# Down projection of a fused cross-attention and expert layer: Strassen's seven products for the second half of each turned group's sum

## The reference, cut to what matters

```python
x = x + attention(layernorm(x), ctx)          # 16 x 112 tokens, 256 wide
h_in = layernorm(x)
# 8 experts, each 256 -> 1024 -> 256, every token goes through all of them
g = jnp.einsum('bsh,ehf->ebsf', h_in, w_gate)
u = jnp.einsum('bsh,ehf->ebsf', h_in, w_up)
h = jax.nn.silu(g) * u
expert_out = jnp.einsum('ebsf,efh->ebsh', h, w_down)
out = jnp.einsum('ebsh,bse->bsh', expert_out, cw)   # cw: one share per token and expert
x = x + out
```

## Time and profile before

| | |
|---|---|
| median of 3 runs | 964.24 us (963.97 to 976.44) |
| the profiled execution | 965.87 us, its span 963.9 us |
| PE busy | 959.1 us, 100% of the span, 5090 matmuls |
| PE weight loads | 890.0 us, 92% |
| DVE, ACT, POOL busy | 541.0, 615.3 and 642.4 us: 56%, 64%, 67% |
| granted TensorE clock | 1.000 |

### The profile page before, as it was taken

How to read it: one execution, slowest core, us unless ns; L and a number is a source line. 1 busy time by engine, 2 the same in 40 slices (tenths; PEclk the granted TensorE clock), 3 DMA queues, 4 the chain that set the end, 5 groups by cost and what they waited for, 6 DMA issues and landing times.

```text
span 963.9 us, 14994 instructions
## 1 busy us (share of the span) xinstructions
PE 959.1 (100%) x5090; PEld 890.0 (92%) x5090; DVE 541.0 (56%) x1024; ACT 615.3 (64%) x1109; POOL 642.4 (67%) x536
## 2 busy tenths in 40 slices
PE   9999999999999999999999999999999999999998
PEld 7999899999999999999999999999999999999998
DVE  4998455455555655556555565555555555555564
ACT  6988556666666566666666566666666565666662
POOL 5899975956566665766565675667565656757564
DMA  7462412311001110111010110111100110112035
GB/s 194 141 157 82 126 60 72 112 46 60 23 23 44 42 64 22 45 41 42 23 44 23 42 63 23 45 41 42 45 23 22 43 61 23 45 42 67 14 53 139
DMA packets 73233, 55.85 MB, mean 58 GB/s; under 512 B 30244, under 2 KB 69485, under 8 KB 73158
## 3 DMA queue, kind: packets, MB, share of 16 engines
q1 hardware_dynamic: 73150, 54.91, 19.6%
q10 hardware_dynamic: 8, 0.00, 0.0%
HBM read 46.58 MB, written 6.48 MB: 55 GB/s over the span
## 4 chain that ended last, share of the span: by engine, by line
PE 97%; DVE 1%; DMA 1%; ACT 0%; issue 0%; SPq 0%; DVEq 0%; ACTq 0%
PE ps L355 95%; PE ps L1874 1%; DMA xf<-in_L_xattn_Wk 1%; PE ps L1910 0%; PE ps L1862 0%; PE ps L1927 0%; DVE early L1371 0%; ACT arena L892 0%; DVE xsacc L1562 0%; PE ps L1953 0%; PE ps L1820 0%; ACT xf L900 0%; ACT xf L892 0%; ACT early L879 0%; DVE ps L1553 0%
## 5 line engine op out<-in xcount | busy, mean ns | idle before, releaser
L355 PE MATMUL ps<-arena 128*128 128x448 f32 (+5 forms) x2064 | 388.3, 339 | 0.1
L355 PEld LDWEIGHTS ps<-arena 128*128 128x128 f32 (+2 forms) x2064 | 343.7, 187 | 21.0 <-DVE arena L366 0.4
L702 POOL TENSOR_TENSOR arena<-shared,arena 128x448 fp32r<-128x448 f32 x196 | 223.8, 1160 | 190.7 <-ACT arena L1107 186.8
L355 PE MATMUL ps<-xc_hi,w_hi 128*128 128x448 f32 x904 | 330.8, 366 | 0.1
L355 PE MATMUL ps<-xc_hi,w_lo 128*128 128x448 f32 x904 | 330.2, 365 | 0.0
L355 PE MATMUL ps<-xc_lo,w_hi 128*128 128x448 f32 x904 | 330.2, 365 | 0.0
L355 PEld LDWEIGHTS ps<-xc_hi,w_hi 128*128 128x128 f32 x904 | 169.8, 188 | 14.0 <-DVE ps L1496 0.5
L355 PEld LDWEIGHTS ps<-xc_hi,w_lo 128*128 128x128 f32 x904 | 169.8, 188 | 13.6
L355 PEld LDWEIGHTS ps<-xc_lo,w_hi 128*128 128x128 f32 x904 | 169.9, 188 | 13.1
L1107 ACT CAST arena<-shared 128x448 fp32r<-128x448 f32 x180 | 102.2, 568 | 108.4 <-DVE shared L1521 44.0
L1553 DVE TENSOR_TENSOR ps<-ps,xf 128x448 f32<-128x448 f32 x104 | 65.6, 631 | 146.3 <-PE ps L355 146.3
(11 more groups left out here) (171 smaller groups left out, 1068.1 us busy)
## 6 DMA issues: line engine op xcount, KB each, us to landing
early<-in_L_ffn_w_down SPq DMA_DIRECT2D x16, 512.0 KB, 3.9
xf<-cw_dram SPq DMA_DIRECT2D x16, 448.0 KB, 4.6
shared<-in_ctx SPq DMA_DIRECT2D x16, 336.0 KB
w_raw<-in_L_ffn_w_gate SPq DMA_DIRECT2D x17, 256.0 KB, 2.7
w_raw<-in_L_ffn_w_up SPq DMA_DIRECT2D x17, 256.0 KB, 3.1
early<-in_L_ffn_w_gate SPq DMA_DIRECT2D x15, 256.0 KB, 2.7
early<-in_L_ffn_w_up SPq DMA_DIRECT2D x15, 256.0 KB, 3.1
xsacc<-in_x SPq DMA_DIRECT2D x8, 224.0 KB, 6.1
```

The costliest lines, as they stand in the source:

```text
L355: ins = nc.tensor.matmul(dst, w, m, start=first and i == 0, stop=last and i == len(passes) - 1, skip_group_check=onto)
L702: nc.gpsimd.tensor_tensor(h[:, 1, j, at:at + TC], tile, h[:, 0, j, at:at + TC].bitcast(fp32), ALU.subtract).then_inc(hid_lo_done, 1)
```

## The change

The hidden tile that quad `n = 2g+1` adds to the down projection of a turned group is a 256 x 896 block (two blocks by two), and so is the result. The change makes its share with Strassen's seven products of three passes, and leaves the first quad's share plain (24 passes).

- **PE.** The four units of a group become nine pieces: `down_1` (3 passes), `down_c11` (3+6), `down_6` (3), `down_7` (3), `down_5` (3) in the even quad, `down_c12` (3+6) and `down_c21_c22` (3+6+6) in the odd one.
- **Sums of the hidden blocks.** DVE makes S3, S1 and S2 (`sums_of_hidden`, each waiting for the one before) once hidden21 is there; hidden21 itself now stays in the PSUM bank `u_x`, and so does S1. POOL makes S4. ACT and POOL split S2, S3 and S4, and ACT and DVE split S1 (`high_sum`, `low_sum`, `low_s1`). Only blocks 11, 12 and 22 of the second quad are split as they are.
- **Sums of the down weights.** POOL makes four (`sum_of_down`); eleven slots instead of eight are split, in two steps (a and b).
- **Keeping and seeding.** ACT seeds one bank with product 1 and keeps products 2 and 5 (`down_seed`, `down_keep2`, `down_keep5`), DVE adds them (`down_c12`, `down_c22`).
- The gate and up weight sums are laid out in seven slots for eight, one weight copy is made whole, the blocks in the arena have other places, and two row tiles of group 1 move to the end of quad 5.

```diff
+            def sums_of_hidden(n):
+                made = 3 * (n // FPAIRS - CP)
+                ve.wait_ge(hid_done, 4 * n + HID21)
+                nc.vector.tensor_tensor(g21, g11, u_x, ALU.subtract).then_inc(s_sum, 1)
+                ve.wait_ge(s_sum, made + S3_MADE)
+                nc.vector.tensor_tensor(u_x, u_x, g22[1], ALU.add).then_inc(s_sum, 1)
+                ve.wait_ge(s_sum, made + S1_MADE)
+                at_least(ve, s_lo_done, made)
+                nc.vector.tensor_tensor(s2_tile, u_x, g11, ALU.subtract).then_inc(s_sum, 1)
...
             def up_seed(n):
                 sc.wait_ge(hid_done, 4 * n)
+                if summed(n - 1):
+                    sc.wait_ge(s1_lo_done, (n - 1) // FPAIRS - CP + 1)
...
+            def high_sum(n, k, src, at):
+                g = n // FPAIRS
+                if k == S4_HI:
+                    sc.wait_ge(s4_made, g - CP + 1)
+                else:
+                    sc.wait_ge(s_sum, 3 * (g - CP) + S2_MADE)
...
+                nc.scalar.copy(single[at][:, 0, :], src).then_inc(s_hi_done, 1)
+            def down_keep5(g):
+                sc.wait_ge(down_prod, piece(g, D_P5))
+                at_least(sc, down_sum, 2 * (g - CP))
+                nc.scalar.copy(d_p5, ps_unit[0]).then_inc(down_kept, 1)
```

ACT's quad, the part that the prediction speaks of:

```diff
+                if odd and turned:
+                    down_keep5(g)
                 gate_seed(n)
                 gate_keep5(n)
                 up_seed(n)
...
+                if summed(n):
+                    high_hidden(n, HID12, g12[n % 2])
+                    activate21(n)
+                    high_hidden(n, HID22, g22[n % 2])
+                else:
+                    high_hidden(n, HID22, g22[n % 2])
+                    high_hidden(n, HID12, g12[n % 2])
+                    activate21(n)
+                    high_hidden(n, HID21, g21)
+                if turn == 3 and hn + 1 < SETS:
+                    high_set(2 * hn + 3)
+                if summed(n):
+                    high_sum(n, S1_HI, u_x, S1_AT)
+                    high_sum(n, S2_HI, s2_tile, S2_AT)
```

DVE's quad:

```diff
                 hidden22(n)
+                if not odd and g in TURNED:
+                    weigh(g, 0)
                 up_c12(n)
                 hidden12(n)
...
-                if not odd and g in TURNED:
-                    weigh(g, 0)
                 hidden21(n)
+                if summed(n):
+                    sums_of_hidden(n)
+                if odd and g in TURNED:
+                    weigh(g, 2)
```

PE's quad and two of the new functions:

```diff
                 if odd and turned:
-                    unit(g, 2)
+                    down_c12(g)
                 gate_6_2(n)
                 if odd and by_tile:
                     down(g, 3)
                 up_6_2(n)
+                if not odd and turned:
+                    down_1(g)
                 gate_7_3(n)
+                if not odd and turned:
+                    down_c11(g)
                 up_7_3(n)
...
                 if not odd and turned:
-                    unit(g, 0)
+                    down_6(g)
                 gate_4(n)
                 up_4(n)
                 if odd and turned:
-                    unit(g, 3)
+                    down_c21_c22(g)
                 if not odd and turned:
-                    unit(g, 1)
+                    down_7(g)
+                    down_5(g)
...
+            def down_5(g):
+                pe.wait_ge(s1_lo_done, g - CP + 1)
+                pe.wait_ge(unit_done, UNITS * (g - CP) + 1)
+                accumulate(ps_unit[0], summed_down(DT1, S1_AT)).then_inc(down_prod, 1)
+            def down_c12(g):
+                pe.wait_ge(s_lo_done, 3 * (g - CP) + S4_LO)
+                pe.wait_ge(down_kept, 3 * (g - CP) + D_KEPT5)
+                accumulate(ps_unit[0], summed_down(DB22, S4_AT) + plain_down(g, 0, 1), first=False, onto=True).then_inc(down_prod, 1)
```

More of the change, by code:

```diff
@@ L147, in xattn_ffn_kernel @@
         cw_all = xf_f[:, 0:CP * TH].rearrange("p (c t) -> p c t", c=CP)
+        d_u2, d_p5 = [xf[:, 4 + i, :] for i in range(2)]
         xc_hi = sb("xc_hi", [P, CP, 7, TC], fp32r)
@@ L797, in _ @@
             plain_low(1, 3)
[L798 removed]
+            low_down_first()
             low_part(0, "s4")
@@ L819, in quad @@
                 hn, turn = n // (CP * FPAIRS), n % (CP * FPAIRS)
-                if n > PLAIN:
-                    low_hidden(n - 1, HID21, g21, 0, TC)
-                if turn == 2:
-                    low_down(hn)
+                if n > PLAIN and not summed(n - 1):
+                    low_hidden(n - 1, HID21, g21)
                 if n == PLAIN:
@@ L1275, in quad @@
                 hn, turn = n // (CP * FPAIRS), n % (CP * FPAIRS)
+                g, odd = n // FPAIRS - 1, n % FPAIRS
+                turned = g in TURNED
+                if turn == 2 and hn == 1:
+                    high_down_a(hn)
+                if odd and turned:
+                    down_keep5(g)
                 gate_seed(n)
@@ L1784, in quad @@
                     turn(1, 1)
-                if not odd and g - 1 not in TURNED:
-                    add_rows(g - 1, 6, ps_r[6])
                 hidden11(n)
@@ new lines, in row_passes, with plain_down @@
+                passes = []
+                for j in range(2):
+                    h, t = pair_of(FPAIRS * g + fp, j), 2 * (2 * fp + 1 - j)
+                    passes += three(h[:, 0, toks], h[:, 1, toks], wd[:, t:t + 2, 0, :], wd[:, t:t + 2, 1, :])
+                return passes
+            def plain_down(g, r, d):
+                passes = []
+                for j, k in enumerate(((HID11, HID12), (HID21, HID22))[r]):
+                    h, t = block_of(FPAIRS * g, k), 2 * (1 - j) + d
+                    passes += three(wd[:, t, 0, :], wd[:, t, 1, :], h[:, 0, :], h[:, 1, :])
+                return passes
@@ new lines, in summed_down, with down_1 @@
+            def summed_down(slot, at):
+                h = single[at]
+                return three(wd[:, slot, 0, :], wd[:, slot, 1, :], h[:, 0, :], h[:, 1, :])
+            def down_1(g):
+                pe.wait_ge(wd_done, g // CP * 2)
+                pe.wait_ge(hid_lo_done, split_count(FPAIRS * g + 1, HID11))
+                if g == CP:
+                    pe.wait_ge(acc_done, RT * CP)
+                    prime(ps_unit[1])
+                at_least(pe, unit_done, UNITS * (g - CP))
+                accumulate(ps_unit[0], summed_down(DB11, A11_AT)).then_inc(down_prod, 1)
@@ L2284, in quad @@
                     down(g, 2)
-                if not odd and g - 1 not in TURNED:
+                if n == PLAIN:
                     down(g - 1, 5)
                 up_1_5(n)
-                if not odd and g - 1 not in TURNED:
+                if n == PLAIN:
                     down(g - 1, 6)
                 if odd and turned:
-                    unit(g, 2)
+                    down_c12(g)
                 gate_6_2(n)
```

405 lines of the change are left out of this document (271 added, 134 removed).

## The result

| | before | changed |
|---|---|---|
| median | 964.11 us (963.8 to 976.44, 4 runs) | **1003.51 us** (1002.8 to 1003.84, 4 runs) |
| ratio | | 1.040, 95% interval 1.037 to 1.044 |
| profiled execution, its span | 965.87, 963.9 us | 1002.8, 1000.7 us |
| PE, DVE, ACT, POOL busy | 959.1, 541.0, 615.3, 642.4 us | 958.4, 634.0, 657.8, 780.0 us |

What follows compares the result with a forecast made beforehand. PE was taken to bound the kernel, with 97% of the last chain. Per group -0.61 (passes) + 0.92 + 0.87 (two waits) = +1.18 us, times 28 = +33 us, giving 997 us against the 964.24 median, range 968 to 1014.

Steps and rivals of the forecast that it cites:

- Passes saved: On PE, three passes fewer in each of 28 groups, 84 x 0.2026 = 17.0 us, all on the path.
- Wait A: PE at the even quad's gate_6_2 waits for gate_seed, behind ACT's casts of S1 and S2: 0.92 us every group.
- Wait B: PE at the odd quad's down_c12 waits for down_keep5, behind the cast of block 21: 0.87 us every group.
- The other waits: At down_7, down_c11, down_5 and up_4: met with 0 to 0.4 us to spare; nothing taken for them.
- the one-time changes: Two tiles of group 1, first split of the larger weight set, sum for waits from group 2: -2 to +3 us.
- The row tiles' moving operand in two pieces: Row tiles' 256 columns now come in two pieces: 336 passes, up to 2 us in all.
- POOL as the bound: Rival: POOL late by 0.5 us at down_c11 and gate_1_5 in each group, 1025 us; chance 18%.
- Load of ACT: ACT gains three casts and three copies, about 3.4 us a group, making it about 78% busy.
- the pace of a pass: Every PE pass was taken to cost 0.2026 us, from the distances between unit starts.
- the prediction's last rival: New gaps drop PE's clock to 1.2 GHz, passes cost twice as much: at worst 732 us more; chance 1%.

Runs made afterwards that it cites:

- Experiment 10: Kernel before with the last pass of units 1, 2 and 3 of each turned group left out (84 passes, result incomplete): 947.34 us, ratio 0.982.
- Experiment 2: Changed kernel with ACT's casts of S1 and S2 moved behind the next quad's gate_seed and gate_keep5: 993.47 us, ratio 1.030.
- Experiment 3: Changed kernel with down_keep5 moved on ACT to the even quad, ahead of the cast of block 12: 992.13 us, ratio 1.028.
- Experiment 4: Experiment 3's kernel with ACT's splits high_down_a (turn 1) and high_set (turn 3) also moved behind up_keep2: 978.77 us, ratio 1.015.
- experiment 7: Changed kernel with one more 448-column GpSimd instruction, result unused, behind the split of S3 in each even quad: 1003.03 us, ratio 1.040.
- Experiment 1: Kernel before with the last three passes of unit 0 left out in each turned group (84 passes, result incomplete): 958.35 us, ratio 0.993.
- experiment 5: Changed kernel with the moves of Experiment 2 and Experiment 4 together: 966.99 us, ratio 1.003.
- experiment 6: Experiment 5's kernel with the second instruction of weigh(g, 2) moved behind low_s1 on DVE: 962.49 us, ratio 0.997.
- experiment 11: Experiment 6's kernel with the second step of the down split moved earlier in turn 2 on ACT and POOL: 958.85 us, ratio 0.995.
- experiment 12: Experiment 11's kernel with DVE making S1 then S2, and GpSimd making S3 as block 22 less S2: 957.79 us, ratio 0.993.
- experiment 8: Experiment 6's kernel with DVE making S1 and S2 first and S3 afterwards, as block 22 less S2 behind low_s1: 1058.12 us, ratio 1.098.

## Why the prediction was right

The forecast was 997 us with 968 to 1014 as range, slower with 76%; it came to 1003.5.

- **Passes saved: right.** Experiment 10 gives 16.8 us for 17.0, and not the 15.9 that the figure of the Trainium skill would give. (Its interval, 16 to 19 us, only just leaves out the 15.9; the distance of the starts, 0.2026 us, does so clearly.)
- **Wait A: right in place and cause, and near in size.** Forecast 0.92 a group, measured 0.75 to 1.07, 23.8 us in 28 against 25.8. Experiment 2 takes it away and leaves B. The chain in the timelines of ACT and DVE (against the earlier trace rows):

```profile
589.10 0.63 DVE L1672 TENSOR_TENSOR ps<-ps,shared 128x448 f32<-128x448 f32 x1
...
592.81 0.63 DVE L1697 TENSOR_TENSOR ps<-shared,ps 128x448 f32<-128x448 f32 x1 [1.08 <-ACT shared L1213]
593.47 0.62 DVE L1703 TENSOR_TENSOR shared<-shared,ps 128x448 f32<-128x448 f32 x1
594.13 0.63 DVE L1705 TENSOR_TENSOR ps<-ps,g_odd 128x448 f32<-128x448 f32 x1
594.79 0.62 DVE L1708 TENSOR_TENSOR shared<-ps,shared 128x448 f32<-128x448 f32 x1
```

```profile
595.45 0.53 ACT L1246 CAST arena<-ps 128x448 fp32r<-128x448 f32 x1 [0.63 <-DVE shared L1708]
595.88 0.57 ACT L1246 CAST arena<-shared 128x448 fp32r<-128x448 f32 x1
596.35 0.54 ACT L1157 COPY ps<-ps 128x448 f32<-128x448 f32 x1
```

  Counted from `down_c12`'s first matmul at 582.57, where the prediction's clock stood at 2.43: up_c22 came 6.53 later (forecast 6.33), hidden21 10.24 (10.03), S1 11.56 (11.35), S1's cast 12.88 (12.67), the seed 13.78 (13.61), PE's restart 14.37 (14.29). Every link has the forecast length to 0.1; the start is 0.2 later, since up's product ended later: the step after the restart is 0.08 longer than a pass, and 30 passes at the slower pace add 0.12.
- **Wait B: right, but for the first two groups.** Forecast 0.87, measured 0.84 to 1.30 in 26 groups, mostly 0.95, and 0.28 in two: 25.2 us against 24.4. Experiments 3 and 4 take it away. The rows: HID21's cast at 581.43, `down_keep5` at 581.90, PE at 582.57; from the restart at 568.83 that is 13.74, for 13.64 forecast.
- **The other waits: right in the change itself, hidden behind A and B.** "Nothing for them" held: only two single waits of 1.3 and 1.2 us came up (3.0 us together by the starts), as large as the +3 that bounded the one-time changes. But with A or B gone, `gate_keep2`, `up_seed` and POOL's down split each turned up, as their thin covers had it. The row tiles' moving operand in two pieces was not tried by itself.
- **POOL as the bound: the rival fell.** POOL is busy for 78%, PE waits for it once, and more work on it costs nothing (experiment 7).
- **Load of ACT: forecast too high, without effect.** ACT's busy time rose by 1.5 us a group (615.3 to 657.8 us) and not by 3.4, DVE's by 3.3 for 3.8; ACT is busy for 66%, not 78%. The rows of a fuller queue overlap more, so adding up their durations overstates it. The sum went by chains and did not use it.
- **What was missing: the pace of a pass was taken as one number.** The sum was -17.0 + 28 x 1.79 = +33. The waits measured 23.8 + 25.2 = 49.0, against 50 in the sum, so they don't explain the 6.5 us by which the forecast was short. Of the passes between 150 and 930 us, 899 of the changed kernel start 0.206 or 0.207 us apart in runs of three and more, against 11 in the kernel before. At 0.2067 for 0.2026, the 888 more are 3.6 us. With the two single waits: -17.0 + 49.0 + 3.6 + 3.0 = +38.6. The medians differ by 39.4, and the profiled spans by 36.8, or 39.0 without the 2.2 us that the kernel before lost at its start. Some 0.4 to 0.8 us stay open. That these terms make up the difference is an account of the trace; the slower pace was not switched off by an experiment. The slow passes are not a plain addition either: wait A is 0.75 to 0.77 us in the twelve groups with a slow stretch ahead of it and mostly 0.90 in the others, so without them the waits would be longer by some 12 x 0.14 = 1.7 us (an estimate). Experiment 7 agrees: 477 slow passes in its trace for 899, waits 1.0 us longer, and the same time. Experiment 1 against 10 shows the effect alone, with the same number of passes and no repeated wait: in the profiled executions, with spans of 951.1 and 945.8 us, the slower pace is 6.4 us over the whole trace, and experiment 10 lost 0.9 us more at its start. The medians are 958.35 and 947.34.

The gain was lost entirely to the order of the queues. With the same products and another order 957.8 us is to be had; of the 10.5 us that still lie between it and experiment 10, some 4.4 are the slower pace (1072 passes of its trace), some 5 the short waits at `up_seed`, and 1.4 a single wait for DVE.

## What to carry to other kernels

Saving work on a full engine pays only if the engines that feed it can keep to their places in the queues: lay out one period of each in-order queue, with the distances of starts from the trace and not the rows' durations, and look for the copy that frees a bank standing behind a cast that waits for somebody else. Moves in ACT's queue alone, at the two waits, were worth 36.5 us here, twice what the algorithm saved. Take one wait away and read the waits again, since the next stands right behind it; and before a sum is moved, look where its operands lie.

## What the runs showed of the hardware

- **Two paces of the same matmul.** At a granted clock of 1.00 a stream of 128x448 passes runs at 0.2026 or at 0.2067 us, and stays at the slower one for up to 330 us (experiment 1, from 577 to 908 us, with no wait of PE in between). In the changed kernel it goes back to 0.2026 after the waits A, as in the rows around 596.94. What starts the slower one stayed open. If every pass ran at it, a time would be 2% longer (an estimate from the two distances), as much as all that the change saves. Slow passes between 150 and 930 us, in the profiled execution of each kernel, and what they cost over 0.2026:

| kernel | passes at 0.2067 | us |
|---|---|---|
| before | 11 | 0.0 |
| changed | 899 | 3.7 |
| experiments 1, 10 | 1608, 11 | 6.6, 0.0 |
| experiments 2, 3, 4, 5 | 1086, 46, 703, 308 | 4.5, 0.2, 2.9, 1.3 |
| experiments 6, 7, 11, 12 | 612, 477, 897, 1072 | 2.5, 2.0, 3.7, 4.4 |

- **A sum on VectorE with both operands in SBUF stood still beside GpSimd's**: 4.01 us in place of 0.62, ending 0.5 us after GpSimd's 4.05 us split, which had started 0.5 us before it. With S3 on GpSimd (experiment 12), whose sums take 1.17, and VectorE's sums in the turned groups with an operand in PSUM, nothing of it is left. Over experiment 8's trace the mean of the 28 sums is 2.71 us. The Trainium skill has this in "SBUF — State Buffer", section "Who interferes with whom": a VectorE instruction with two SBUF inputs contends with a GpSimd instruction that reads SBUF; the shared ports are an exclusive lock, and the order of issue decides who is blocked. The trace agrees: here GpSimd came first, and VectorE's instruction ended a sum's length after it.
- **The clock fell after long gaps and not after short ones.** With some 0.9 us twice in 28 us the granted clock stayed 1.00, and in experiment 8 passes went on at 0.20 us behind starts 1.6 us apart. There, after a gap of 3.7 us, it was 0.50 (the level of 1.2 GHz) in the next 4 us, 0.68 in the 4 after that, and 1.00 again then. At the lower level a pass took 0.373 us, 1.84 times the 0.2026 at the upper one and not twice, as the prediction's last rival had it. The Trainium skill ("TensorE: Matmul & The Clock Gate", "HAM oscillation") has short gaps harmless and long ones followed by the lower level, and this agrees with both.
- **A start can differ by 2 us.** The profiled execution of the kernel before was 1.8 us above its median, and lost 2.2 us in its first 13 us against the changed kernel's. The prediction made its sum on that execution and then took its forecast from the median, which was right.
